# Pacing one scatter stream and moving additions, bias products and summing turns in a one-core graph-transformer kernel

## The chip, the cores and the metric

The kernel runs on one core of a Trainium2 chip, in fp32. The metric is the device time of one execution in microseconds (us), as the median of the runs of each kernel.

## The reference

A graph of 6250 nodes with 256 features and 100,000 weighted edges goes through two layers. `_L0_gnn_ref` and `_L1_gnn_ref` sum rows of neighbours, `_L0_mix_ref` is a linear attention with two layernorms, `_L1_mix_ref` a stack of four transformer layers with a linear attention, `_L0_ffn_ref` a mixture of 32 experts (top 1), `_L1_ffn_ref` one of 6 experts of width 256 (top 2, mixed by a softmax of the two scores).

```python
xn = _layernorm(x)
x = x + _L0_gnn_ref(xn, edge_index, edge_weight, ...) + _L0_mix_ref(xn[None], ...)[0]
x = x + _L0_ffn_ref(_layernorm(x)[None], ...)[0]
xn = _layernorm(x)
x = x + _L1_gnn_ref(xn, src, dst, deg_isqrt[:, None], weight) + _L1_mix_ref(xn[None], ...)[0]
x = x + _L1_ffn_ref(_layernorm(x)[None], ...)[0]     # sum over 2 of gate * (h2 @ W3[e] + b3[e])
```

## The kernel before, in words

The nodes are 50 tiles of T = 125 tokens. A loop iteration takes a pair of slots, each slot two tiles (250 tokens, a "chunk"), so NP = 13 iterations cover the NC = 25 chunks, the last with one slot only. Each engine has an instruction stream of its own; they meet at semaphores, and `Steps`/`KINDS` count the named steps of a phase (a name with ">" is done one iteration ahead).

The order of the work is this.

- **Sort, scatter(0).** DVE works out where every edge goes, twice (once per graph layer). POOL then sends the edges of the first sort to `scratch_sorted0` with 782 indirect DMAs of 128 records of 8 bytes (`scatter`, L975; EC = 782). At most `FLYING` of them are on their way: number c waits for c - FLYING to have landed. Beside this, PE, ACT and DVE do layer 0's attention (phases A0, B0).
- **Records.** SP loads the sorted records into `srec` (the names of tiles are those of the rows: `sb_srec`), DVE splits them into row numbers and targets (`take_records`, L1673 to L1676).
- **C0**, 25 iterations: POOL gathers 128 rows of `scratch_xn` at a time (`gather`, L982, NS = 880, a ring of RING = 8 tiles `sb_rows`), DVE makes a one-hot matrix of each, PE sums by a matmul with it (L2297), DVE adds the sum to its block (L1692). Beside it go the graph layer's MLP and the 32 experts. After every third gather (`BESIDE` = 3) POOL puts one scatter of the second sort, 293 in all; the other 489 follow in a tail behind C0, there with a memset of a spare tile behind each (`sb_rest`, L1010) as a pause. The tail's end is a load of `srec` (L1015) and a memset of the sums' 125 x 12850 tile (L1017).
- **A1.n, B1.n**, n = 0 to 3: the four layers. A1.n makes the context, B1.n the rest. From B1.1 on, each iteration carries three "turns" of the second graph sum: a turn is 8 gathers (L982), the one-hots (L1627), 16 matmul instructions (L2282), 4 additions (L1637) into `SUM[1]` (`sb_FREE`). 110 turns are due; B1.1 and B1.2 do 36 each, B1.3 the rest, two of them in its last iteration, which has one slot. DVE takes the records at the start of B1.1 (L1673 again).
- **C1**, written out over pairs j with the steps skewed (`C1_PE`, `C1_ACT`, `C1_DVE` list the names). DVE forms h = xn1 + sum (L2052, tile KT, pair j+2), PE turns it by transposes (L2227, 8 of them), multiplies by the graph weight (L2236), DVE adds it to x2 + state, the sum "xa" (L2113, tile TM), giving x3 (L2037) and its layernorm z (L2091), PE multiplies z by the router (L2682, L2689), DVE picks the two experts and works out the rows, POOL scatters z to those rows of `scratch_zs` (L1030, 8 indirect DMAs per pair). z has a ring of two buffers (`ZR`): z(j+1) waits for the scatters of pair j-1, in its buffer, to have landed.
- **Experts**, 54 tiles of 256 rows sorted by expert: PE turns the tile (L2735), two hidden layers (L2722), two matmuls that put in the bias of the chosen expert (L2763, out of a one-hot column), the output layer (L2767).
- **End.** POOL gathers the results of the two experts of each token (L1050, 100 indirect DMAs of 125 rows), DVE adds them times the gate (L2217), SP stores.

What each step waits for in the code: `scatter` holds `pool.wait_ge(scattered[e][c % FLYING], 16 * (c // FLYING))`; the first gather needs `srec_taken` 4, that is the whole scatter(0) landed, loaded and taken; the first gather of the second pass needs `srec_taken` 8. A gather also needs its ring slot back from PE (`row_free`).

## Time and profile before

| what | us |
|---|---|
| median of 3 runs | 7180.03 (7178.28 to 7499.05) |
| the profiled execution's own time | 7168.51 |
| its span, first to last instruction | 7166.8 |
| PE busy | 5509.7 |
| DVE busy | 3387.8 |
| POOL busy | 3803.2 |

The rows below are from the profiled execution, so times within it add up to 7168.51, not to the median. In the rows of a timeline a line is its start, its length, and in brackets how long the engine had been idle before it and what ended that. In grouped rows "xN" is the number of instructions, then busy us, the mean of one in ns, and the idle time before them with what ended it.

### The profile page before, as it was taken

To read this page: it belongs to the slowest core of one execution; us is meant where nothing else is said; L and a number is where in the kernel's file an instruction comes from. 1 tells how busy PE (TensorE), PEld (TensorE's weight loads), DVE (VectorE), ACT (ScalarE), POOL (GpSimd) and SP (SyncE) were. 2 spreads that over 40 slices of the span, in tenths; PEclk is the share of its full clock that TensorE was granted. 3 is DMA by queue.
4 is the path that set the end of the run, shared out by engine and by line. 5 is a ranking of instruction groups with operands and counts; after the bars stand their busy time and mean duration, and the time that the engine had idled before them with its cause. 6 is when DMAs were issued, how large, how long until landed. Compare 5 with 4: busy or idle time off the path is not lost.

```text
span 7166.8 us, 87343 instructions
## 1 busy us (share of the span) xinstructions
PE 5509.7 (77%) x24743; PEld 4508.0 (63%) x24743; DVE 3387.8 (47%) x10012; ACT 1297.9 (18%) x2949; POOL 3803.2 (53%) x4056
## 2 busy tenths in 40 slices
PE   0356673017999999999889999999998999965990
PEld 0245552015666666667778878888887878854880
DVE  8776664013444444443744554446444644456222
ACT  0011110000111111111422331124111411111330
POOL 0655556766666666667888725530554045535006
PEclk9987886557999999999999999999999999976995
DMA  1122220022222222232110122221322122443224
GB/s 37 39 74 67 62 65 22 1 61 73 83 80 82 81 82 80 82 79 46 49 28 18 35 71 79 80 71 54 83 82 76 43 76 82 77 105 92 80 71 114
DMA packets 327764, 477.28 MB, mean 67 GB/s; under 512 B 106708, under 2 KB 248254, under 8 KB 327470
## 3 DMA queue, kind: packets, MB, share of 16 engines
q0 software_dynamic: 161136, 262.61, 14.8%
q1 hardware_dynamic: 166334, 211.17, 9.5%
q8 instruction: 133, 2.18, 0.1%
q14 instruction: 161, 1.32, 0.1%
HBM read 370.96 MB, written 102.33 MB: 66 GB/s over the span
## 4 chain that ended last, share of the span: by engine, by line
PE 60%; another core or an unknown queue 8%; DVE 7%; issue 7%; DMA 3%; POOL 2%; DVEq 1%; ACT 1%; SPq 1%; POOLq 0%; ACTq 0%
PE bank L2236 13%; PE bank L2247 13%; PE bank L2297 6%; PE bank L2282 5%; PE bank L2463 5%; PE bank L2442 5%; PE bank L2722 3%; PE bank L2588 2%; PE bank L2227 2%; PE bank L2767 1%; POOL scratch_zs L1030 1%; PE bank L2445 1%; POOL sb_HT L1050 1%; DMA sb_work_QT<-scratch_q 1%
## 5 line engine op out<-in xcount | busy, mean ns | idle before, releaser
L982 POOL DMA_INDIRECT sb_rows<-scratch_xn,sb_row_of x1760 | 1734.2, 985 | 1849.8 <-PE bank L2282 939.8
L975 POOL DMA_INDIRECT scratch_sorted<-sb_FREE x1564 | 1604.0, 1026 | 890.8 <-issue 372.6
L2247 PE MATMUL bank<-sb_work_FT,sb_W 128*128 128x250 f32 x4400 | 1012.7, 381 | 16.3 <-ACT sb_work_FT L1059 11.5
L1059 ACT ACTIVATE sb_HT<-bank,sb_cols 128x250 f32<-128x250 f32 x1333 | 548.7, 467 | 2358.1 <-PE bank L2445 751.5
L2247 PEld LDWEIGHTS bank<-sb_work_FT,sb_W 128*128 128x128 f32 x4400 | 849.6, 194 | 131.7 <-ACT sb_work_FT L1059 16.5
L2297 PE MATMUL bank<-sb_rows,sb_work_TM 128*125 128x257 f32 x1760 | 528.7, 424 | 500.7 <-DMA sb_rows<-scratch_xn,sb_row_of 372.4
L2236 PE MATMUL bank<-sb_W,sb_HT 128*125 128x256 f32 x4000 | 889.0, 380 | 3.1 <-ACT sb_HT L1059 2.7
L2236 PEld LDWEIGHTS bank<-sb_W,sb_HT 128*125 128x125 f32 x4000 | 751.0, 188 | 118.3 <-ACT sb_HT L1059 4.4
L2297 PEld LDWEIGHTS bank<-sb_rows,sb_work_TM 128*125 128x125 f32 x1760 | 335.3, 203 | 591.3 <-issue 505.7
L1692 DVE TENSOR_TENSOR sb_STATE<-sb_STATE,bank 125x257 f32 x440 | 185.1, 421 | 971.0 <-PE bank L2297 663.7
L1637 DVE TENSOR_TENSOR sb_FREE<-sb_FREE,bank 125x257 f32 x440 | 186.1, 423 | 746.3 <-PE bank L2282 449.8
L2282 PE MATMUL bank<-sb_rows,sb_work_TM 128*125 128x257 f32 x1760 | 454.4, 401 | 22.9 <-DVE sb_FREE L1637 7.0
L2442 PE MATMUL bank<-sb_work_FT,sb_FREE 128*128 128x250 f32 x1600 | 463.5, 414 | 9.9 <-issue 9.2
L2463 PE MATMUL bank<-sb_FREE,sb_HT 128*125 128x256 f32 x1600 | 408.6, 401 | 0.0
L2236 PE MATMUL bank<-sb_W,sb_work_FT 128*125 128x256 f32 x1600 | 390.3, 403 | 19.9 <-ACT sb_work_FT L1059 19.9
L2282 PEld LDWEIGHTS bank<-sb_rows,sb_work_TM 128*125 128x125 f32 x1760 | 337.5, 197 | 102.2 <-issue 27.6
L2236 PEld LDWEIGHTS bank<-sb_W,sb_work_FT 128*125 128x125 f32 x1600 | 315.6, 201 | 76.6 <-ACT sb_work_FT L1059 20.2
L2442 PEld LDWEIGHTS bank<-sb_work_FT,sb_FREE 128*128 128x128 f32 x1600 | 305.7, 203 | 90.4 <-issue 30.3
L2463 PEld LDWEIGHTS bank<-sb_FREE,sb_HT 128*125 128x125 f32 x1600 | 308.3, 198 | 56.3 <-issue 9.0
L1059 ACT ACTIVATE sb_work_FT<-bank,sb_cols 128x250 f32<-128x250 f32 x400 | 192.3, 567 | 827.5 <-PE bank L2227 811.2
L1050 POOL DMA_INDIRECT sb_HT<-scratch_ys,sb_srec x100 | 120.6, 1206 | 412.9 <-DMA scratch_ys<-sb_work_KT 382.7
L1683 DVE TENSOR_SCALAR sb_work_TM<-sb_iota_t,sb_srec 128x125 f32<-128x125 f32 x880 | 284.4, 378 | 0.0
(363 smaller groups left out, 6933.9 us busy)
## 6 DMA issues: line engine op xcount, KB each, us to landing
sb_rows<-scratch_xn,sb_row_of POOLq DMA_INDIRECT x1760
scratch_sorted<-sb_FREE POOLq DMA_INDIRECT x1564
scratch_qT<-sb_work_QF SPq DMA_DIRECT2D x100, 250.0 KB
sb_work_QF<-scratch_qT SPq DMA_DIRECT2D x100, 250.0 KB
sb_work_XC<-in_x SPq DMA_DIRECT2D x50, 250.0 KB
sb_work_ZT<-scratch_xn SPq DMA_DIRECT2D x50, 250.0 KB
sb_W<-in_L_mix_W SPq DMA_DIRECT2D x9, 1024.0 KB
sb_work_XC<-scratch_zs SPq DMA_DIRECT2D x28, 256.0 KB, 2.7
```

Of the source, the lines that this page charges most:

```text
L975: nc.gpsimd.indirect_dma_start(out=sorted_d[e], out_offset=bass.IndirectOffsetOnAxis(ap=pos[e][0:n, c:c + 1], axis=0), in_=rec[e][0:n, 2 * ...
L982: nc.gpsimd.indirect_dma_start(out=rows[:, t % RING, 0:D], out_offset=None, in_=table, in_offset=bass.IndirectOffsetOnAxis(ap=row_of[:, t: ...
L1050: nc.gpsimd.indirect_dma_start(out=GY[j % YRING][:, t, k, :], out_offset=None, in_=ys_d, in_offset=bass.IndirectOffsetOnAxis(ap=Y_AT[:, 2 ...
L1059: return nc.scalar.activation(dst, source, func, **k)
L1683: nc.vector.tensor_scalar(onehot[:, u % RING, :], iota_t[:], srec[:, u, 0:1], srec[:, u, 1:2], ALU.is_equal, ALU.mult).then_inc(onehot_mad ...
L2236: ins = nc.tensor.matmul(dst[:, t, :], source[:, k, T * t:T * t + T], w[:, k, :], start=(begin and k == k0 and t == 0), stop=(end and k == ...
L2247: ins = nc.tensor.matmul(dst[:, b, :], w[:, k0 + k, 128 * (b0 + b):128 * (b0 + b) + 128], source[:, k, :], start=(n == 0), stop=(n == 2 * ...
L2282: nc.tensor.matmul(PSUMS[u // 2 % 2][0:T, 0:D + 1], onehot[:, u, :], rows[:, u, :], start=(u % 2 == 0), stop=(u % 2 == 1)).then_inc(row_fr ...
L2297: nc.tensor.matmul(PSUMS[g % 2][0:T, 0:D + 1], onehot[:, u % RING, :], rows[:, u % RING, :], start=(u % 2 == 0), stop=(u % 2 == 1)).then_i ...
L2442: nc.tensor.matmul(acc[:, b, :], w0_up[:, k, at:at + 128], FT[j % 2][:, k, :], start=(k == 0), stop=False)
L2463: ins = nc.tensor.matmul(acc[:, t, :], HT[:, j % 2, (2 * p + b) % 4, T * t:T * t + T], w0_down[:, 2 * p + b, :], start=False, stop=(p == 7 ...
L2722: ins = nc.tensor.matmul(whole(dst)[:, b, :], w[:, k, 128 * b:128 * b + 128], source[:, k, :], start=(k == 0), stop=(k == 1))
```

## The change

1. `FLYING` goes from 2 to 4, and every scatter(0) gets a pause behind it (`pause`, a memset of 128 x 320 as in the tail). `BESIDE` goes from 3 to 4: 220 scatters of the second sort beside C0, 562 in the tail.
2. The summing turns begin with the third iteration of B1.1; the last iterations of B1.1 and B1.2 carry three turns too, so 110 are still done. `take_records(1)` moves from before B1.1 to its second begin.
3. B1.3 drops the layernorm statistics behind its result, and adds x2 to the state instead (loaded there); C1 has no h and no xa on DVE. PE adds xn1 and the sum itself: 16 matmuls with the identity that accumulate in pairs, in place of 8 transposes. PE's graph product of pair j+2 now waits for DVE's x3 of pair j+1.
4. `ZR` has three buffers: z(j+1) waits for the scatters of pair j-2.
5. The bias matmuls leave the expert tiles. Behind the last tile PE turns a matrix of gates (50 tiles of 125 x 8, placed by five DVE operations during the experts), ACT copies it, and PE multiplies it by the biases; DVE adds that to the state, one addition of 125 x 512 per chunk ahead of its four gate additions. Two route steps go.
6. `Y_AT` and the gathers of results have 128 rows instead of 125.

```diff
-BESIDE = 3
-FLYING = 2
+BESIDE = 4
+PACED = EC
+FLYING = 4
...
-C1_DVE = (named(1, "x3", "stats", "mean") + named(2, "h") + named(0, "logit", "lmax", "lsub") + named(1, *RSQRT)
+C1_DVE = (named(1, "x3", "stats", "mean") + named(0, "logit", "lmax", "lsub") + named(1, *RSQRT)
...
+TURNS_FROM = {"B1.1": 2}
...
+LAST_TURNS = TURNS[f"B1.{LAYERS - 1}"] - (_turns - NS // RING)
...
+            def pause(n):
+
+                if n:
+                    pool.wait_ge(rested, n)
+                nc.gpsimd.memset(rest[:], 0.0).then_inc(rested, 1)
+
             for c in range(EC):
                 scatter(0, c)
+                if c < PACED:
+                    pause(c)
...
+                    if phase == "B1.1" and isinstance(i, int) and i == TURNS_FROM[phase] - 1:
+                        dve.wait_ge(sums_zeroed, 1)
+                        take_records(1)
...
-                if j + 2 < NP:
-                    for s in (slots_of(j + 2)):
-                        wait(dve, (xn1_read[s], 16 * (j + 3)))
-                        ins = nc.vector.tensor_tensor(KT[s], ZT[s], SUM[1][:, 4 * (j + 2) + 2 * s:4 * (j + 2) + 2 * s + 2, 0:D],
-                                                      ALU.add)
-                    ins.then_inc(*c1_dve.add("h", j + 2))
...
-                    wait(pe, c1_dve.done("h", j + 2))
                     for s in (slots_of(j + 2)):
-                        ins = turn_tok(pfeat(PA[s]), KT[s])
+                        wait(pe, (xn1_read[s], 16 * (j + 3)))
+                        sums = SUM[1][:, 4 * (j + 2) + 2 * s:4 * (j + 2) + 2 * s + 2, 0:D]
+                        for k in range(2):
+                            for t in range(2):
+                                for n, part_of in enumerate((ZT[s], sums)):
+                                    ins = nc.tensor.matmul(pfeat(PA[s])[:, k, T * t:T * t + T],
+                                                           part_of[:, t, 128 * k:128 * k + 128], ident[0:T, 0:T],
+                                                           start=(n == 0), stop=(n == 1))
                     ins.then_inc(*c1_pe.add("hT", j + 2))
                     wait(pe, c1_act.done("hT", j + 2))
+                    if j + 1 >= 0:
+                        wait(pe, c1_dve.done("x3", j + 1))
...
-                    if j >= 1:
-                        wait(dve, (z_scattered[(j + 1) % 2], 64 * sum(len_of(i) for i in range((j + 1) % 2, j, 2))))
+                    if j + 1 >= ZN:
+                        wait(dve, (z_scattered[(j + 1) % ZN], 64 * sum(len_of(i) for i in range((j + 1) % ZN, j + 1, ZN))))
...
                     for u in range(2):
-                        nc.tensor.matmul(y[:, u, :], chosen[:, t:t + 1].to_broadcast([NEXP1, 128]), bexp1,
-                                         start=(u == 0), stop=False, skip_group_check=True)
...
             for j in range(NC):
+                dve.wait_ge(bias_made, j + 1)
+                nc.vector.tensor_tensor(XM[:, 2 * j:2 * j + 2, :], XM[:, 2 * j:2 * j + 2, :], ptok(BIASED[j % 4]), ALU.add)\
+                    .then_inc(gate_added, 1)
                 dve.wait_ge(y_gathered[j % YRING], 64 * (j // YRING + 1))
```

POOL from the end of scatter(0) to the first gathers of C0, before (`scratch_sorted0` and `1` are the two sorts' outputs, `sb_rows` the ring of gathered rows):

```order
L975 DMA scratch_sorted0<-sb_FREE 112640x2 x782
L994 MEMSET sb_W1 32x2048
L929 AFFINE_SELECT sb_W1<-sb_W1 32x2048 x2
L982 DMA sb_rows<-scratch_xn0,sb_row_of 128x256 x3
L975 DMA scratch_sorted1<-sb_FREE 112640x2
```

and of the change, from the last scatter of the first sort on:

```order
L991 DMA scratch_sorted0<-sb_FREE 112640x2
L1008 MEMSET sb_rest 128x320
L1018 MEMSET sb_W1 32x2048
L945 AFFINE_SELECT sb_W1<-sb_W1 32x2048 x2
L998 DMA sb_rows<-scratch_xn0,sb_row_of 128x256 x4
L991 DMA scratch_sorted1<-sb_FREE 112640x2
```

Each of the 782 scatters now has a memset behind it, and the scatters in C0 stand behind four gathers instead of three.

PE in C1, one pair before (`sb_HT` the router's hidden layer, `sb_work_KT` is h, `sb_work_FT` its transpose, the `bank` numbers are PSUM banks):

```order
L2689 MATMUL bank6<-sb_W0,sb_HT 125x6 x4
L2227 MATMUL bank0<-sb_ident,sb_work_KT 128x125 x4
L2227 MATMUL bank3<-sb_ident,sb_work_KT 128x125 x4
L2236 MATMUL bank1<-sb_W0,sb_work_FT 125x256 x4
L2236 MATMUL bank4<-sb_W0,sb_work_FT 125x256 x4
L2668 MATMUL bank7<-sb_srec,sb_lower 125x32
```

and of the change. Sixteen products stand for one pair in the place of the eight transposes, eight per slot; the fence has the last two of them and what follows:

```order
L2705 MATMUL bank3<-sb_ident,sb_work_ZT 128x125
L2705 MATMUL bank3<-sb_ident,sb_FREE 128x125
L2279 MATMUL bank1<-sb_W0,sb_work_FT 125x256 x4
L2279 MATMUL bank4<-sb_W0,sb_work_FT 125x256 x4
L2719 MATMUL bank7<-sb_srec,sb_lower 125x32
```

The transposes of the DVE's sum are replaced by products of xn1 (`sb_work_ZT`) and of the sums (`sb_FREE`) in turn into one bank.

PE in the expert loop, one tile before (`sb_work_XC` the loaded tile, `sb_work_FT`, `sb_work_QF` and `sb_work_QT` the three layers' inputs, `sb_srec` holds the one-hot column):

```order
L2735 MATMUL bank0<-sb_ident,sb_work_XC 128x128 x4
L2722 MATMUL bank4<-sb_work_FT,sb_W0 128x256 x4
L2722 MATMUL bank2<-sb_work_QF,sb_W0 128x256 x4
L2717 TENSOR_LOAD sb_srec
L2717 ISA x2
L2763 MATMUL bank7<-sb_W1,sb_srec 128x256 x2
L2767 ISA
L2767 MATMUL bank7<-sb_FREE,sb_work_QT 128x256 x2
L2767 ISA
L2767 MATMUL bank7<-sb_FREE,sb_work_QT 128x256 x2
```

and of the change:

```order
L2786 MATMUL bank3<-sb_ident,sb_work_ZT 128x128 x4
L2773 MATMUL bank1<-sb_work_FT,sb_W0 128x256 x4
L2773 MATMUL bank5<-sb_work_QF,sb_W0 128x256 x4
L2768 TENSOR_LOAD sb_srec
L2768 ISA x2
L2815 ISA
L2815 MATMUL bank6<-sb_FREE,sb_work_QT 128x256
L2815 ISA
L2815 MATMUL bank6<-sb_FREE,sb_work_QT 128x256 x3
```

The two bias products are gone from every tile, and nothing stands in their place there.

## Rows read from the trace of the kernel before

**Rows 1.** The page: busy time and share, and the sum matmuls of C0.
```profile
PE 5509.7 (77%) x24743; PEld 4508.0 (63%) x24743; DVE 3387.8 (47%) x10012; ACT 1297.9 (18%) x2949; POOL 3803.2 (53%) x4056
...
L2297 PE MATMUL bank<-sb_rows,sb_work_TM 128*125 128x257 f32 x1760 | 528.7, 424 | 500.7 <-DMA sb_rows<-scratch_xn,sb_row_of 372.4
```

**Rows 2.** Busy time by stretch: PE, PEld, DVE, ACT, POOL, then clock, DMA share, GB/s.
```profile
1172.00:1518.00 346.00, 1.62 (x2) 0.08 (x2) 13.95 (x12) 0.00 (x0) 261.54 (x270) 0.50 0.02 1
1640.00:3240.00 1600.00, 1441.54 (x5928) 1075.85 (x5926) 686.02 (x2589) 203.77 (x480) 1038.60 (x1072) 0.91 0.30 81
3617.00:4008.00 391.00, 383.60 (x1815) 335.18 (x1813) 162.26 (x496) 103.50 (x242) 342.06 (x500) 0.99 0.07 15
...
6374.00:6590.00 216.00, 145.72 (x599) 117.13 (x599) 152.97 (x692) 34.54 (x85) 106.07 (x88) 0.70 0.35 103
6630.00:7000.00 370.00, 369.95 (x1716) 297.62 (x1716) 80.65 (x210) 122.63 (x270) 0.00 (x0) 1.00 0.23 74
7010.00:7160.00 150.00, 0.00 (x0) 0.00 (x0) 40.90 (x98) 0.00 (x0) 117.00 (x97) 0.50 0.48 125
```

**Rows 3.** Groups by line, POOL, stretches 240:700, 700:1160, 3331:4083 (two).
```profile
L975 POOL DMA_INDIRECT scratch_sorted<-sb_FREE x222 | 240.2, 1082 | 218.5 <-DMA scratch_sorted<-sb_FREE 170.6 <-issue 47.9
...
L975 POOL DMA_INDIRECT scratch_sorted<-sb_FREE x234 | 265.7, 1135 | 196.0 <-DMA scratch_sorted<-sb_FREE 139.9 <-issue 56.1
...
L975 POOL DMA_INDIRECT scratch_sorted<-sb_FREE x464 | 457.8, 987 | 117.1 <-issue 73.5 <-DMA scratch_sorted<-sb_FREE 43.5
L1010 POOL MEMSET sb_rest<- 128x320 f32 x465 | 178.2, 383 | 0.3
```

**Rows 4.** Timeline of POOL: scatter(0)'s end, C0's first gather, C0's end, the clearing behind the tail.
```profile
1516.92 1.04 POOL L975 DMA_INDIRECT scratch_sorted<-sb_FREE  x1 [0.30 <-issue]
1532.09 1.04 POOL L982 DMA_INDIRECT sb_rows<-scratch_xn,sb_row_of  x1 [0.17 <-issue]
...
3292.04 0.99 POOL L975 DMA_INDIRECT scratch_sorted<-sb_FREE  x1 [0.30 <-issue]
...
4085.81 10.83 POOL L1017 MEMSET sb_FREE<- 125x12850 f32 x1
```

**Rows 5.** Timeline of DVE: the records taken, for C0 and for B1.1.
```profile
1523.70 0.62 DVE L1673 TENSOR_SCALAR sb_row_of<-sb_srec 128x880 f32<-128x880 f32 x1 [331.50 <-DMA sb_srec<-scratch_sorted]
...
4214.68 0.62 DVE L1673 TENSOR_SCALAR sb_row_of<-sb_srec 128x880 f32<-128x880 f32 x1 [0.89 <-DMA sb_work_QF<-scratch_qT]
```

**Rows 6.** Timeline of PE: iterations of B1.0 and B1.1, B1.3's last iteration.
```profile
3652.27 4.07 PE L2247 MATMUL bank<-sb_work_FT,sb_W 128*128 128x250 f32 x18 [0.67 <-ACT sb_work_FT L1059]
...
3684.86 4.49 PE L2247 MATMUL bank<-sb_work_FT,sb_W 128*128 128x250 f32 x20 [0.58 <-ACT sb_work_FT L1059]
...
4305.48 3.62 PE L2236 MATMUL bank<-sb_MM,sb_work_QF 128*125 128x256 f32 x16
...
4352.05 3.62 PE L2236 MATMUL bank<-sb_MM,sb_work_QF 128*125 128x256 f32 x16
...
6307.89 0.94 PE L2282 MATMUL bank<-sb_rows,sb_work_TM 128*125 128x257 f32 x2 [0.79 <-DMA sb_rows<-scratch_xn,sb_row_of]
```

**Rows 7.** C1: timeline of PE, then DVE's groups by line, 6374:6590.
```profile
6466.02 6.68 PE L2236 MATMUL bank<-sb_W,sb_work_FT 128*125 128x256 f32 x16 [1.15 <-ACT sb_work_FT L1059]
...
6483.92 1.05 PE L2227 MATMUL bank<-sb_ident,sb_work_KT 125*128 125x125 f32 x8
...
L2052 DVE TENSOR_TENSOR sb_work_KT<-sb_work_ZT,sb_FREE 125x512 f32<-125x512 f32 x19 | 12.7, 705 | 0.3
L2091 DVE TENSOR_SCALAR sb_work_QT<-sb_STATE,sb_MV,sb_RY 125x256 f32<-125x256 f32 x22 | 7.6, 409 | 23.5 <-DMA scratch_zs<-sb_work_QT,sb_srec 23.5
L2091 DVE TENSOR_SCALAR sb_W<-sb_STATE,sb_MV,sb_RY 125x256 f32<-125x256 f32 x20 | 6.9, 409 | 13.6 <-DMA scratch_zs<-sb_W,sb_srec 13.6
```

**Rows 8.** Experts 6630:7000 and the end: groups by line.
```profile
L2763 PE MATMUL bank<-sb_W,sb_srec 6*128 6x256 f32 x216 | 60.7, 400 | 0.0
...
L1050 POOL DMA_INDIRECT sb_HT<-scratch_ys,sb_srec x97 | 117.0, 1206 | 29.6 <-issue 26.5 <-DVE sb_STATE L2217 3.1
```

More of the change, by code:

```diff
@@ L270, in pairs, with pairs_next @@
     body(NP - 1, (0,))
-def pairs_next(engine, begin, body):
+def pairs_next(engine, begin, body, phase=None):
     begin(0, (0, 1))
-    body(0, (0, 1), (0, 1))
-    with engine.Fori(1, NP - 2) as i:
+    written_out = max(1, TURNS_FROM.get(phase, 0))
+    for i in range(written_out):
+        body(i, (0, 1), (0, 1))
+    with engine.Fori(written_out, NP - 2) as i:
         body(i, (0, 1), (0, 1))
@@ L492, in build @@
         tilesT, beganT, endedT = (carve(1, 8) for _ in range(3))
[L493 removed]
+        ended = carve(NX, NEXP1)
         exp_row, real, tile_in = (carve(NX, 1) for _ in range(3))
@@ L555, in build @@
         gate_added, out_stored = sem("gate_added"), sem("out_stored")
+        gates_placed, gates_turned, gates_copied, bias_made = (
+            sem(n) for n in ("gates_placed", "gates_turned", "gates_copied", "bias_made"))
         routing_cleared, y_placed = sem("routing_cleared"), sem("y_placed")
-        ROUTE_STEPS = ["tiles", "whole", "began", "ended", "done", "begun", "chosen", "row", "real", "in", "rel", "in0",
+        ROUTE_STEPS = ["tiles", "whole", "began", "ended", "done", "row", "real", "in", "rel", "in0",
                        "last", "exp_of", "in_of"]
@@ L853, in load_b1 @@
                                      .rearrange("u p (k n) -> p (u k) n", k=2)).then_inc(q_loaded.sems[s], 16)
+                    if phase == f"B1.{LAYERS - 1}":
+                        for s in slots:
+                            if not first(i):
+                                wait(sp, dve_done.done(phase, "xa", i - 1, s))
+                            sp.dma_start(XC[s], tiles(x2_d)[:, bass.ds(4 * i + 2 * s, 2), :]).then_inc(x2_read.sems[s], 16)
                 pairs_late(sp, load_b1, load_for_next)
@@ L882, in _ @@
                     sp.dma_start(dst, source).then_inc(weights_loaded["exp_rest"], 16)
-                wait(sp, c1_dve.done("xa", j))
-                for s in (slots_of(j + 1)):
-                    load_x2(j + 1, s)
             weight_loads["exp_rest"] = 16 * 2 * NEXP1
-            for s in range(2):
-                sp.wait_ge(z_scattered[s], 64 * sum(len_of(j) for j in range(s, NP, 2)))
+            for q in range(ZN):
+                sp.wait_ge(z_scattered[q], 64 * sum(len_of(j) for j in range(q, NP, ZN)))
             sp.wait_ge(pads_scattered, 16 * 2 * NEXP1)
@@ L1007, in _ @@
                 scatter(1, c)
-                if c > ahead_of:
-                    pool.wait_ge(rested, c - ahead_of)
-                nc.gpsimd.memset(rest[:], 0.0).then_inc(rested, 1)
+                pause(PACED + c - ahead_of)
             for mark in all_scattered(1):
@@ L1258, in _ @@
                     relu_tile(b, "b", H2, PC, 1)
+            for q in range(NP):
+                n = T * 2 * len_of(q)
+                act.wait_ge(gates_turned, q + 1)
+                if q >= 2:
+                    act.wait_ge(bias_made, 2 * (q - 1))
+                move(GT[q % 2][:, 0:n], PA[q % 2][0:8, 0:n]).then_inc(gates_copied, 1)
         @block.vector
@@ L1968, in body_b1 @@
                             .then_inc(*dve_done.add(phase, "b2", slots, s))
+                    if phase == f"B1.{LAYERS - 1}":
+                        for s in slots:
+                            self_wait(phase, "b2", i, s)
+                            wait(dve, x2_read.done(phase, i, s))
+                            nc.vector.tensor_tensor(state(i, s), state(i, s), XC[s], ALU.add)\
+                                .then_inc(*dve_done.add(phase, "xa", slots, s))
+                        return
                     for s in slots:
@@ L2033, in body_c1 @@
                 if 0 <= j + 1 < NP:
-                    wait(dve, c1_dve.done("xa", j + 1))
                     wait(dve, c1_pe.done("gnn", j + 1))
@@ L2179, in _ @@
                 dve.wait_ge(weights_loaded[name], weight_loads[name])
-            for s in range(2):
-                dve.wait_ge(z_scattered[s], 64 * sum(len_of(j) for j in range(s, NP, 2)))
+            for q in range(ZN):
+                dve.wait_ge(z_scattered[q], 64 * sum(len_of(j) for j in range(q, NP, ZN)))
             of_tile = {}
```

117 lines of the change are left out of this document (72 added, 45 removed).

## The prediction

> **What bounds the kernel now.** The page first: PE is busy 77% of the span, POOL 53%, and one line of PE, the sum matmuls of C0, has waited 372.4 us once for gathered rows [rows 1]. No engine is full throughout, so each stage has to be read for its own limit.
>
> The table of stretches gives it [rows 2]. In 1172:1518 PE does 1.62 us of work and POOL 261.54: nothing goes on but scatter(0). The timelines show how it ends: last scatter at 1516.92, DVE takes the records at 1523.70 after 331.50 idle, the first gather is at 1532.09 [rows 4, 5]. In C0 (1640:3240) PE has 1441.54 of 1600, at clock 0.91; in the attention layers (3617:4008) 383.60 of 391; in the experts (6630:7000) all of it. [...] In the end (7010:7160) POOL has 117.00 of 150 and nobody else comes near [rows 2].
>
> So: POOL bounds from about 1165 to 1532 and the last 150 us, PE nearly all the rest, and C1 a chain. A saving on POOL in A1 or B1, or on DVE there, is worth nothing.
>
> **The change, part by part.** The terms are added to the profiled execution's own 7168.51 us. The comparison runs of the same kernel have a median of 7180.03, 11.5 more; I give the sum as it comes from the profile.
>
> *Scatter(0).* While the attention runs, 222 scatters take 240.2 + 218.5 us, 2.07 each; 234 take 265.7 + 196.0, 1.97 each [rows 3]. Of this 170.6 and 139.9 are waits for a landing: with two in flight, number c waits for c - 2. Four in flight leave 4 x 1.7 = 6.8 us for a landing where now some 4 are given, so I take those waits as gone. The added memset costs 0.383 [rows 3], and the gap before a scatter is then 73.5/464 = 0.16 [rows 3]. Scatter 1.11 (mean of the two stretches) + 0.16 + 0.38 = 1.65; I take 1.70, for contention. In quiet, the tail of before shows 457.8 + 73.5 + 178.2 us for 464, without its landing waits: 1.53. Now: 42 scatters are done by 240 us as before, 925/1.70 = 544 by 1165, and the other 196 take 300 us: the end is at 1465, not 1517. C0 starts with it: **-52**. Bounds: at 1.65 the end is 1439 (-78); if the waits stay as they are, 2.02 each, it is 42 + 458, then 282 x 1.53 = 431, end 1596 (+79). What the memset costs DVE in A0 and B0 has 370 us of idle PE behind it.
>
> [...] In 3617:4008 POOL did 250 memsets beside 250 scatters and PE still had 383.60 of 391 [rows 2]; nothing shows that memsets harm a neighbour. [...]
>
> *C0.* From 1532.09 to 3292.04 are 25 iterations of 70.4 us [rows 4]. POOL has 1038.60 us of work in 1600 [rows 2] and loses 73 scatters; it has room either way. PE's rest, 158 us in 1600, is spread over waits that the views don't put on gathers. Only the first 100 us, while the ring fills, go by POOL's pace: a fourth gather in place of a scatter now and then, 6 scatters of 1.3 us. **-8**, bounds 0 and -158 (the whole of PE's rest in that stretch gone).
>
> *Tail of scatter(1).* 562 instead of 489. Before, 1.62 each with all waits: (457.8 + 117.1 + 178.2)/464 [rows 3]; without landing waits 1.53. From 3292 it ends between 4152 and 4204; then the load is issued and the sums are cleared, over at 4085.81 + 10.83 = 4096.6 [rows 4], 13 us behind the tail's end (3292 + 489 x 1.62 = 4084). DVE needed the records at 4214.68 [rows 5]; now one half iteration later, about 4231. Margin 14 to 66 us: **0**.
>
> *B1 turns.* An iteration without turns takes 3684.86 - 3652.27 = 32.6 us, one with three 4352.05 - 4305.48 = 46.6 [rows 6]: a turn is 4.66. Six turns leave the first two iterations of B1.1 (-28) and six enter two last iterations with one slot. There a turn has half as much beside it: B1.3's last one, with two turns, waits for gathers in between (0.79 in the row [rows 6]). I take 6.3 each, +38. **+10**, bounds 0 and +25.
>
> *B1.3 and C1's start.* B1.3 loses the statistics and gains two additions per iteration on DVE, which has slack. C1's first loads are two of 250 KB instead of four: **-3**.
>
> *C1.* The stretch 216 us holds 88 scatters, 11 pairs: 19.6 us per pair. DVE waits 23.5 + 13.6 = 37.1 us in it for a scatter to have left the z buffer, 3.4 per pair [rows 7]. With three buffers that goes, and POOL's 8 scatters (106.07/88 + 0.30 = 1.5 each, 12 per pair) don't bound. DVE is left with 16.2, less two pairs of 0.7 (L2052, and L2113 of the same form) [rows 7]: 13.4. PE: busy 13.2 per pair at clock 0.70, so some 9.3 at full clock. The 16 added products have 16 x 125 columns, about as many as the 8 products of 256 columns that take 3.62 at full clock and 6.68 at half [rows 6, 7]; less the transposes' 1.05, +2.5. Four waits for ACT of 1.15 [rows 7] give 4.6. Sum 16.4 at full clock, 18.6 + 5.5 + 4.6 = 28.7 at half. PE becomes C1's bound. I take 16.4 with a little at half: 12 periods x -3.2 = **-38**. Bounds: -12 x 6.2 = -74 (DVE alone) and 12 x 9.1 = +109 (all at half clock).
>
> [...]
>
> *Experts.* Four instructions per tile leave, 60.7 us as recorded [rows 8], 4/32 of 6.85 us per tile by count, which is 46 over 54 tiles. PE is full there [rows 2] and DVE and ACT, 80.65 and 122.63 of 370, have room. I take **-57**. The new transposes and products at the end fill a wait that POOL's gathers set; DVE gets one addition of 125 x 512 per chunk, 0.7 by the like one in rows 7, where it has 40.90 busy of 150.
>
> *End.* 97 gathers of 125 rows take 1206 ns each [rows 8], the indirect DMAs of 128 rows 987 in the tail [rows 3]. The 0.30 between them stays: 100 x 0.22 = **-22**, bounds 0 and -25.
>
> Sum: -52 - 8 + 0 + 10 - 3 - 38 - 57 - 22 = -170, so 7168.5 - 170 = **6998 us**.
>
> **Rivals.**
>
> *(a) The pause costs more than the flights give.* If landings aren't what holds POOL but the transfers' own pace, the period stays 2.02 with the memset inside: +79 instead of -52, 7129. For it: 1.97 to 2.07 while the DMAs are busy. Against: 310 us of the idle is named as a landing wait, and only 104 as issue.
>
> *(b) C1 at half clock.* +109 instead of -38: 7145; half of it 7072. For it: clock 0.70 now, four waits per pair. Against: PE is busier per pair than before (12 of 16 instead of 13 of 20).
>
> *(c) C0's rest goes.* If PE's 158 us come from late gathers after all, a third less scatter work in between lets most go: -110 instead of -8, 6896. Against: POOL is no more than 65% busy.
>
> *(d) The bias products weren't the bound.* If the tiles wait for their loads once PE is faster, -57 becomes 0: 7055. Against: DMA share 0.23.
>
> *(e) The tail comes late, slower than before.* DVE takes the records at the second begin of B1.1, and everything behind it on DVE and PE waits. From 1.65 us per scatter (4231 - 13 - 3292 = 926 over 562) this bites, at 5.6 us per 0.01. At 2.07, as beside A0 [rows 3], the tail ends 3292 + 1163 = 4455, 237 late: 7235, slower. For it: no more than 0.03 between 1.623 and 1.65. Against: beside A1 the transfers are few (15 GB/s [rows 2]), and four flights take the landing waits off.
>
> **How the numbers follow.** Chances: the forecast 0.60, (a) 0.09, (b) 0.14, (c) 0.07, (d) 0.05, (e) 0.05. The forecast's own range is 6955 to 7040. The whole range leaves out the far half of (c), most of (a) and (e) and the worst of (b): 6920 to 7110. A measurement of this kernel tells about 2% from no change, a bound of 7025 on the profile's own base. Forecast and (c) lie mostly below it, with 27 us to spare: faster 0.62. (a), (b), (d) and what the forecast misses by more than that: same 0.35. A case that is 2% slower needs (e) and (a) together: 0.03.
>
> **What would show it.** Right: scatter(0) ends near 1465, without landing waits in A0 and B0; the first gather near 1480; tail's load of records before 4180 in old time; C1's groups of scatters 16 to 17 us apart with PE, not the z ring, as releaser and a clock above 0.9; expert tiles at 5.8 us; final gathers 1.3 us apart. Wrong: landing waits that stay in scatter(0), a granted clock of 0.5 through C1, an idle DVE ahead of the second taking of records, or a C0 iteration off 70 us by more than 1.

## The result, and the profile after

The changed kernel takes 6965.57 us (median of 4 runs, 6947.83 to 6978.54); the kernel before took 7181.57 in the same comparison. The ratio is 0.9699, its 95% interval 0.9672 to 0.9726: 3.0% faster. Some runs of the kernel before are slow ones (here 7499.05 us, one of four, and three of seven on the second chip below), and neither the ratios nor the medians below rest on such runs. The profiled execution of the changed kernel took 6978.54 us, against 7168.51: 190 us less, where 170 had been forecast.

The page of the changed kernel, busy time and the sum matmuls of C0 (now line 2340), answers to [rows 1]:

```profile
PE 5457.0 (78%) x24977; PEld 4497.6 (64%) x24977; DVE 3425.7 (49%) x9891; ACT 1306.8 (19%) x2962; POOL 4109.6 (59%) x4911
...
L2340 PE MATMUL bank<-sb_rows,sb_work_TM 128*125 128x257 f32 x1760 | 511.2, 417 | 322.9 <-DMA sb_rows<-scratch_xn,sb_row_of 276.5
```

The wait for C0's first gathered rows is still the longest of PE, 276.5 instead of 372.4 us: 63 of the 96 us less come from an earlier C0, the rest from PE ending layer 0's attention later. POOL is busier by 306 us; the 855 memsets more, at about 0.39 us each, account for it. The stretches that answer to [rows 2], of the changed kernel (PE, PEld, DVE, ACT, POOL, clock, DMA share, GB/s):

```profile
1172.00:1458.00 286.00, 14.97 (x54) 10.79 (x54) 32.46 (x61) 2.19 (x4) 253.83 (x375) 0.52 0.03 5
1580.00:3100.00 1520.00, 1378.73 (x5852) 1045.84 (x5852) 677.63 (x2541) 203.27 (x476) 949.82 (x984) 0.94 0.30 83
6297.00:6492.00 195.00, 141.89 (x851) 122.56 (x850) 137.00 (x696) 35.02 (x87) 116.47 (x100) 0.88 0.35 96
6520.00:6815.00 295.00, 295.00 (x1469) 259.88 (x1468) 81.79 (x211) 119.63 (x264) 0.00 (x0) 1.00 0.28 89
6830.00:6960.00 130.00, 45.98 (x116) 26.14 (x114) 49.57 (x109) 5.19 (x9) 91.45 (x94) 0.50 0.46 138
```

C1's clock has gone from 0.70 to 0.88; the experts are as full as before and shorter; in the last stage POOL is busy 91.45 us of 130, where it was 117.00 of 150.

POOL's scatters of the first sort, groups by line in 240:700 and 700:1160, answer to [rows 3]:

```profile
L991 POOL DMA_INDIRECT scratch_sorted<-sb_FREE x273 | 289.1, 1059 | 65.0 <-issue 41.9 <-DMA scratch_sorted<-sb_FREE 23.1
...
L991 POOL DMA_INDIRECT scratch_sorted<-sb_FREE x271 | 295.9, 1092 | 55.6 <-issue 43.6 <-DMA scratch_sorted<-sb_FREE 11.9
```

273 in 460 us is one every 1.69 us, and the landing waits are down from 170.6 and 139.9 us to 23.1 and 11.9. The timelines of POOL (the last scatter, the first gather, the clearing of the sums) and of DVE (the second taking of records) answer to [rows 4, 5]:

```profile
1458.09 0.88 POOL L991 DMA_INDIRECT scratch_sorted<-sb_FREE  x1 [0.17 <-issue]
...
1469.01 1.00 POOL L998 DMA_INDIRECT sb_rows<-scratch_xn,sb_row_of  x1 [4.00 <-DVE sb_row_of L1705]
...
4020.40 10.84 POOL L1039 MEMSET sb_FREE<- 125x12850 f32 x1
...
4129.39 0.61 DVE L1702 TENSOR_SCALAR sb_row_of<-sb_srec 128x880 f32<-128x880 f32 x1
```

The last thing that the second taking of records waits for was done 98 us before it (4031.2 to 4129.4), so the longer tail costs nothing.

Where did the 190 us come from? The starts of the first or last instruction of each stage, read from the views of single lines, give this table. The right half is from two later runs of the same two kernels on another chip, told below.

| stretch | before | after | difference | before, 4th chip | after, 4th chip | difference |
|---|---|---|---|---|---|---|
| start to first gather of C0 | 1532.1 | 1469.0 | -63.1 | 1520.8 | 1462.3 | -58.5 |
| to C0's last sum matmul | 1774.1 | 1704.3 | -69.8 | 1502.9 | 1488.9 | -14.0 |
| to the last addition of a turn | 3004.8 | 3066.3 | +61.5 | 2901.4 | 2920.5 | +19.1 |
| to the first scatter of z | 63.4 | 56.7 | -6.7 | 62.8 | 55.9 | -6.9 |
| to the last scatter of z | 232.2 | 195.6 | -36.6 | 230.2 | 195.6 | -34.6 |
| to the first expert matmul | 22.2 | 22.0 | -0.2 | 22.0 | 22.1 | +0.1 |
| to the last expert matmul | 372.9 | 305.4 | -67.5 | 374.1 | 305.3 | -68.8 |
| to the last gate addition | 159.0 | 152.5 | -6.5 | 160.0 | 134.8 | -25.2 |

So on the first chip three terms were far from the forecast: C0 gave 70 instead of 8, the turns cost some 60 instead of 10, and the end gave 6.5 instead of 22. The first two nearly cancel. The experiments went after these three, and after the two halves of the first edit.

### The profile page after: what moved, and what is told of

Same layout as the page of the kernel before. It is cut to its first block, busy times and chain, and to the rows that moved or that the text cites. A ratio compares the mean times of both kernels' runs of the same rounds, so it can differ in the third digit from the quotient of the medians.

```text
span 6976.8 us, 88468 instructions
## 1 busy us (share of the span) xinstructions
PE 5457.0 (78%) x24977; PEld 4497.6 (64%) x24977; DVE 3425.7 (49%) x9891; ACT 1306.8 (19%) x2962; POOL 4109.6 (59%) x4911
## 4 chain that ended last, share of the span: by engine, by line
PE 60%; POOL 15%; DVE 8%; issue 7%; DMA 5%; another core or an unknown queue 4%; DVEq 1%; ACT 1%; SPq 0%; ACTq 0%; POOLq 0%
PE bank L2279 14%; PE bank L2290 13%; POOL scratch_sorted L991 10%; PE bank L2325 6%; PE bank L2340 5%; PE bank L2506 5%; PE bank L2485 4%; POOL sb_rest L1008 4%; DMA scratch_sorted<-sb_FREE 3%; PE bank L2773 3%; PE bank L2631 3%; PE bank L2270 2%; PE bank L2815 1%; DMA sb_rows<-scratch_xn,sb_row_of 1%
## 5 line engine op out<-in xcount | busy, mean ns | idle before, releaser
L2340 PE MATMUL bank<-sb_rows,sb_work_TM 128*125 128x257 f32 x1760 | 511.2, 417 | 322.9 <-DMA sb_rows<-scratch_xn,sb_row_of 276.5
L1008 POOL MEMSET sb_rest<- 128x320 f32 x1344 | 523.6, 390 | 1.0
L2485 PE MATMUL bank<-sb_work_FT,sb_FREE 128*128 128x250 f32 x1600 | 439.5, 398 | 0.3 <-issue 0.3
L2279 PE MATMUL bank<-sb_W,sb_work_FT 128*125 128x256 f32 x1600 | 366.2, 385 | 21.2 <-ACT sb_work_FT L1081 13.2
L2279 PEld LDWEIGHTS bank<-sb_W,sb_work_FT 128*125 128x125 f32 x1600 | 297.9, 190 | 69.7 <-issue 13.2
L2506 PEld LDWEIGHTS bank<-sb_FREE,sb_HT 128*125 128x125 f32 x1600 | 304.7, 196 | 56.7 <-issue 10.7
L1072 POOL DMA_INDIRECT sb_HT<-scratch_ys,sb_srec x100 | 97.9, 979 | 355.2 <-DMA scratch_ys<-sb_work_KT 314.8
```

The costliest lines, as they stand in the source:

```text
L1008: nc.gpsimd.memset(rest[:], 0.0).then_inc(rested, 1)
L2279: ins = nc.tensor.matmul(dst[:, t, :], source[:, k, T * t:T * t + T], w[:, k, :], start=(begin and k == k0 and t == 0), stop=(end and k == ...
L2340: nc.tensor.matmul(PSUMS[g % 2][0:T, 0:D + 1], onehot[:, u % RING, :], rows[:, u % RING, :], start=(u % 2 == 0), stop=(u % 2 == 1)).then_i ...
L2485: nc.tensor.matmul(acc[:, b, :], w0_up[:, k, at:at + 128], FT[j % 2][:, k, :], start=(k == 0), stop=False)
L2506: ins = nc.tensor.matmul(acc[:, t, :], HT[:, j % 2, (2 * p + b) % 4, T * t:T * t + T], w0_down[:, 2 * p + b, :], start=False, stop=(p == 7 ...
```

## The experiments

Twelve kernels were run, four to a chip; each chip also ran the kernel before. The kernel before took 7142 us (median) on the second chip, 6783.09 on the third, 6787.21 on the fourth, where the first had 7180. This difference of 5.0 to 5.5% is larger than the change, and it turned out to sit just where the forecast had missed. So I compare stages within a chip where I can, else between the first and the second or between the third and the fourth, which are alike, and across chips only ratios.

**Fewer scatters beside C0, alone and taken back (second chip).**

```diff
-BESIDE = 3
+BESIDE = 4
```
in the kernel before, and `BESIDE = 3` in the changed kernel.

> The kernel before with BESIDE = 4 alone (one scatter of the second sort behind every fourth gather, 562 of them in the tail). C0, from its first sum matmul to its last, took 1768 us before and 1698 in the changed kernel. Theory A, fewer scatters between the gathers give this: C0 takes about 1700 here, the whole is 55 to 70 us faster than before, 7110 to 7125. Theory B, the four flights give it (a scatter no longer holds POOL until an earlier one has landed): C0 stays within 10 us of 1768, the whole within 15 us of before.

> The changed kernel with BESIDE = 3. Theory A: C0 goes back to about 1765 and the whole is 55 to 70 us slower than the changed kernel, about 7030. Theory B: C0 stays at 1698 within 10, the whole at 6966 within 15. If both parts count, each of the two runs shows some half of the 70.

The kernel before with `BESIDE = 4` took 7065.56 us, ratio 0.9894 (0.9854 to 0.9933), and C0, from its first sum matmul to its last, 1680.9 us. The changed kernel with `BESIDE = 3` took 6982.13, ratio 0.9775 (0.9741 to 0.9808), C0 1750.2. All three kernels of this chip with `BESIDE = 4` (this one and those of the next two experiments) have 1675.5 to 1685.5, so C0 is 65 to 75 us shorter with it; on the first chip it was 1768.2 before and 1697.5 in the changed kernel. Theory A stands: the number of scatters beside C0 is what counts, at 0.9 to 1.0 us for each of the 73. The flights (how many scatters may be on their way) show no effect on C0: the 1680.9 is with two, the other two kernels have four.

**The turns put back (second chip).**

```diff
-TURNS_FROM = {"B1.1": 2}
+TURNS_FROM = {}
```
with the records taken before B1.1 and the last iterations of B1.1 and B1.2 without turns, as in the kernel before.

> The changed kernel with the summing turns where they were before (from B1.1's first iteration, none in the last iterations of B1.1 and B1.2). From the last sum matmul of C0 to the last addition of a turn before took 3004.8 us, in the changed kernel 3066.3, 61 more, of which the moved turns were to give 10. Theory C, the moved turns cost it: this stretch goes back to about 3005 and the whole is 55 to 60 us faster than the changed kernel, about 6907. Theory D, the iterations fall into a 43 us or a 47.4 us pattern by chance, whatever the turns: the stretch is shorter by the 10 to 25 us that the turns themselves cost, and the count of 47 us iterations does not go back to 20 of 36.

It took 6898.92 us, ratio 0.9661 (0.9623 to 0.9699), the fastest of that chip. The stretch from C0's last sum to the last turn took 3014.0 us, against 3044.0 and 3047.1 in the two kernels of this chip with moved turns. So moving them costs 30 to 33 us here, half of theory C's 61 and more than theory D's 10 to 25. Where it goes can be read from the starts of the iterations, on the first chip: the last, single-slot iterations of B1.1 and B1.2 take 18 to 20 us more each (234.4 and 233.1 instead of 214.8 and 214.7 from the iteration before to the first of the next layer), +38; the first two of B1.1 take 33.5 and 32.6 instead of 45.0 and 46.4, -25. Most of the rest is slow iterations. On these chips a B1 iteration takes either some 43 or some 47 us, and the three kernels with moved turns had 24, 22 and 21 of 34 at over 45.5, the three others 19, 21 and 19 of 36. PE's timeline of the changed kernel shows what a slow one has:

```profile
5049.45 1.74 PE L2270 MATMUL bank<-sb_ident,sb_work_ZT 125*128 125x125 f32 x8 [2.69 <-DVE sb_work_ZT L1336]
5051.29 3.00 PE L2325 MATMUL bank<-sb_rows,sb_work_TM 128*125 128x257 f32 x8
```

PE waits 2.69 us for DVE's normalised tile; then the granted clock is 0.50 (in 5050:5053; 0.99 in the 2 us before, 1.00 from 5054 on), the 8 transposes take 1.74 instead of 1.05 us and the next 8 matmuls 3.00 instead of 1.90. The wait and the half clock make 4.5 us, about what lies between the two kinds. Why DVE's tile is late in them is not shown.

**No pause, four flights (second chip).**

```diff
-PACED = EC
+PACED = 0
```

> The changed kernel with four flights but no pause behind the scatters of the first sort. Theory E, the pause pays for itself by spacing the scatters: without it scatter(0) is not sooner than 1458 us. Theory F, the pause only adds its 0.38 + gap and the landing waits are gone by the flights: a scatter takes 1.11 + 0.30 = 1.41 instead of 1.69 beside A0 and B0 and 1.26 behind, so scatter(0) ends at about 172 + 50 x 1.39 + 925 / 1.41 and is done near 1250 us, C0 starts some 200 us earlier, bounded by the end of B0 at about 1170, and the whole is some 200 us faster than the changed kernel. In between, landing waits with four flights decide: at 1.97 us as before, the end is 1517 again and the whole is 60 us slower.

It took 7500.4 us, ratio 1.0501 (1.0466 to 1.0536): 5% slower than the kernel before. Neither theory had this. The scatters did go faster, the last was issued at 1239.6, as F said. But C0's first gather came at 2038.5. Beside the scatters layer 0's attention nearly stood still. The stretch 240:700 of this run, then of the changed kernel:

```profile
240.00:700.00 460.00, 68.11 (x199) 47.96 (x200) 71.22 (x172) 10.75 (x22) 348.47 (x346) 0.58 0.06 13
```
```profile
240.00:700.00 460.00, 242.36 (x1078) 207.25 (x1078) 324.46 (x709) 68.57 (x140) 394.95 (x546) 0.79 0.23 65
```

PE did 68 us of work instead of 242, the DMAs moved 13 GB/s instead of 65, and the DMA engines were busy 6% of the time: they were not full. The timeline of the run without pauses shows who was held up:

```profile
653.62 0.16 DVE L1302 TENSOR_TENSOR sb_RT<-sb_RY 125x4 f32<-125x4 f32 x1 [2.63 <-issue]
653.86 1.10 POOL L991 DMA_INDIRECT scratch_sorted<-sb_FREE  x1 [0.30 <-issue]
655.10 0.59 ACT L1081 ACTIVATE sb_work_FT<-bank 128x500 f32<-128x500 f32 x1 [56.14 <-remote]
655.27 1.09 POOL L991 DMA_INDIRECT scratch_sorted<-sb_FREE  x1 [0.30 <-issue]
...
657.11 0.16 DVE L1303 TENSOR_TENSOR sb_RT<-sb_RT,sb_RV 125x4 f32<-125x4 f32 x1 [3.34 <-issue]
```

The little operations of DVE's inverse root, each 0.16 us long and waiting only for the one before it, start 2.1 to 3.5 us apart, about two scatters, where in the kernel before they follow every 0.27. The profile puts the gaps before them (1.95 to 3.34 us in 653:677) down to "issue" and names no data and no DMA that they wait for; meanwhile POOL issues indirect DMAs back to back, mostly 0.30 us apart. What is late in the step from one instruction to the next is not shown, nor whether the issuing does it or the landings, which come as densely. ACT and PE have long gaps too (56.14 us and, at 655.81, 51.32), with no releaser named; that they have the same cause is likely, not shown. In the kernel before, the waits for a landing, 170.6 and 139.9 us in two stretches of 460 [rows 3], had broken POOL's stream; in the changed kernel, with four flights, they are 23.1 and 11.9, and the pause has to do it. The memsets have a price of their own on DVE. One of its operations in 240:1160, in the kernel before and in the changed one:

```profile
L1307 DVE TENSOR_SCALAR sb_work_ZT<-sb_work_XC,sb_MV,sb_RY 125x256 f32<-125x256 f32 x50 | 17.5, 412 | 2.5 <-DVE sb_RY L1275 2.1 <-issue 0.2
```
```profile
L1336 DVE TENSOR_SCALAR sb_work_ZT<-sb_work_XC,sb_MV,sb_RY 125x256 f32<-125x256 f32 x50 | 25.3, 564 | 2.5 <-DVE sb_RY L1304 2.1 <-issue 0.2
```

It takes 564 ns instead of 412, and a little one of 125x4 (now L1300) 535 instead of 193; without pauses they take 420 and 170. The TENSOR_TENSOR operations of the inverse root stay at 163 to 166, and the TENSOR_SCALAR of the same line and shape that reads a PSUM bank at 537 and 538. DVE's 1714 instructions in 160:1458 take 747 us instead of 698, and PE's last work ahead of C0's sums ends at 1209.1 instead of 1177.7; how much of that is the memsets' part is not separated. Why some operations become longer beside the memsets and others do not is not shown. It costs the whole nothing, since PE then still waits 267 us for C0's rows. Without the pauses DVE did 71 us of work in 460 instead of 324.

**Pause with two flights (third chip).**

```diff
-FLYING = 4
+FLYING = 2
```

> The changed kernel with two scatters in flight and the pause kept. Theory K, with the pause two flights do as well as four: scatter(0) ends within 10 us of 1458. Theory L, the flights took the landing waits off: at 1.97 to 2.07 us per scatter beside A0 and B0 it ends at about 1590, the whole is 130 us slower than the changed kernel; if a part of the waits stays, in between. C0 should stay at 1676 to 1698 in both.

It took 6783.49 us, ratio 0.9995 (0.9985 to 1.0004): all that the rest of the change gains is lost. Scatter(0)'s last was issued at 1655.3 instead of 1452. POOL's group in 240:700:

```profile
L991 POOL DMA_INDIRECT scratch_sorted<-sb_FREE x203 | 216.0, 1064 | 166.0 <-DMA scratch_sorted<-sb_FREE 140.0 <-issue 25.8 <-DVE sb_STATE L1401 0.2
```

The landing waits are all back, 140.0 us, 0.69 per scatter, and the pause comes on top: 2.27 us per scatter, more than theory L's 2.07 (it had taken the pause to lie inside the waits). C0 took 1480.9, as in the kernels of this chip with four flights (1481.6 and 1483.4): flights do nothing there. With the run before, the first edit is settled: pause and flights are worth something only together. C0's first gather is 54 to 63 us earlier with both than with neither (1467.7 and 1470.6 against 1524.8 on the second chip), 145 us later with the pause alone (1666.2 against 1520.8 on the fourth), 514 later with the flights alone (2038.5 against 1524.8).

**Pauses elsewhere (third and fourth chip).** All with the turns where they were; a pause is the same memset behind the instruction.

```diff
-                gather(1, xn1_d, t)
+                gather(1, xn1_d, t); pause(PACED + EC - ahead_of + t)
```

> The changed kernel with the turns where they were before (as in the run of the moved turns), and a pause (the memset of 128 x 320) behind each of the 880 gathers of the second sum. Theory G, POOL's DMA instructions back to back hold up the semaphores and instructions of the other engines, and the 47 us iterations of B1.1 to B1.3 come from that: with the pause most of the 36 iterations fall to 43 us, the stretch from the last sum of C0 to the last turn is 50 to 90 us shorter than 3014. Rival H, the 47 us pattern is PE's and DVE's own: nothing changes within 15 us, or the stretch grows because 24 gathers of 1.5 us leave less room.

```diff
-                    scatter(1, t // BESIDE)
+                    scatter(1, t // BESIDE); pause(PACED + t // BESIDE)
```

> The same base, with a pause behind each of the 220 scatters in C0. Theory G: C0 (1675 in the base) shrinks, by up to 60 us, since each scatter would hold PE up less. Rival I, a scatter in C0 costs its own POOL time, because gathers are late by it: the pause adds up to 220 x 0.24 us, C0 takes 1690 to 1730.

```diff
-                            .then_inc(y_gathered[j % YRING], 16)
+                            .then_inc(y_gathered[j % YRING], 16); pause(PACED + EC - ahead_of + 4 * j + 2 * t + k)
```

> The same base, with a pause behind each of the 100 final gathers. A gather then takes 1.50 instead of 1.255 us, 25 us more of POOL. In the changed kernel ACT copied two of its 13 gate tiles 28 and 15 us after PE had turned them, with no releaser that the profile names, and POOL then waited 9.3 us. Theory G: those gaps go, POOL never waits, and the final stage takes 149.7 + 25 - (9 to 14), 160 to 166 us. Rival J, the gaps are instruction loads of ACT: they stay where they are, and the stage takes 170 to 175.

The ratios are 0.9776 (0.976 to 0.9793) with the pause in B1, 0.9730 (0.9714 to 0.9746) in C0, 0.9735 (0.9719 to 0.9752) at the end. What was to be cured did not occur on this chip: without a pause its B1 iterations take 42.4 us, nearly every one, and C0 1483.4. So each pause only cost its time: B1's stretch 2947.8 instead of 2904.6 and 2907.1 in the other two, C0 1498.4 instead of 1483.4, the end 158.3 instead of 135.8. For theory G in C0 and B1 these runs decide nothing; that a pause is not free is what they show. A fourth kernel had the pauses in C0 and in B1 together:

> The turns where they were, with a pause behind each scatter in C0 and each gather of the second sum. Theory G (POOL's DMA instructions back to back hold up the other engines) gives on a chip like the first C0 and B1 at the pace of the third chip or near it: C0 down by 100 or more from 1676 and B1's iterations at 43 to 44, the whole 100 us or more faster than the changed kernel. Rival H: C0 within 20 us of 1690, B1's iterations still at 43 and 47. On a chip like the third both say 15 us more in C0 and 40 more in B1, as in the two runs that had one of the pauses each.

It fell on the fourth chip, like the third, and took 6643.81 us, ratio 0.9787 (0.9771 to 0.9804), C0 1497.1: the price again, and no verdict.

**The two kernels again, on the fourth chip.**

> The kernel before, unchanged, profiled on the same chip as the next three. The chips differ: on the first and second one the kernel before took 7180 and 7164 us, on the third 6783, and there C0 with BESIDE = 4 took 1482 to 1498 us and the iterations of B1 42.4, instead of 1676 to 1698 and 43 to 47. Theory M, the chip decides C0 and B1 and nothing else: on a chip like the third C0 is near 1510 here and B1's iterations 42.4, every other stage as in the rows of before; on a chip like the first all is as in them.

> The changed kernel, unchanged, on that chip. Scatter(0) should end at 1453 to 1458 on any chip, C1 be some 37 us shorter than in the run of before, the experts 67. C0: 53 to 87 us shorter than before on a chip like the first; on one like the third, where it runs at PE's pace (98% busy), no more than 20 to 30. From C0's last sum to the last turn: 13 us longer than before on a chip like the third (the turns alone), 30 to 60 on one like the first.

6787.25 and 6594.49 us; the second's ratio is 0.9714 (0.9697 to 0.9730). The stages are in the right half of the table above. Theory M stands, with one addition: besides C0 and B1 the end differs, 134.8 instead of 152.5 us in the changed kernel, while it takes 160.0 and 159.0 in the kernel before. All others agree within 5 us, but for the start (6.7 to 11). C0's stretches of the two kernels, before first:

```profile
1640.00:2960.00 1320.00, 1290.88 (x5799) 990.52 (x5800) 662.81 (x2507) 204.44 (x475) 1003.75 (x1038) 1.00 0.35 95
```
```profile
1580.00:2900.00 1320.00, 1294.20 (x5850) 998.68 (x5849) 674.87 (x2533) 206.32 (x480) 942.83 (x979) 1.00 0.36 95
```

PE is 98% busy at full clock in both, so scatters taken out of C0 give only 14 us. On the first chip the same code had PE at 90% with clock 0.91 [rows 2]. Rows that come late are not the reason there. A gather is 32 packets of 4096 bytes; past the first 40 gathers PE stood 34 times for more than 0.3 us ahead of a sum matmul, 55 us in all, and each time the last packet of its rows had ended 4.2 us or more before. On the fourth chip it stood so 17 times, 19 us, and the middle one of these was 0.39 us behind the packet.

The end on the first chip, ACT's and POOL's timeline of the changed kernel, and ACT's on the fourth:

```profile
6904.67 0.58 ACT L1081 ACTIVATE sb_work_FT<-bank 8x500 f32<-8x500 f32 x1 [33.02 <-remote]
...
6910.72 0.95 POOL L1072 DMA_INDIRECT sb_HT<-scratch_ys,sb_srec  x1 [9.32 <-DVE sb_STATE L2251]
```
```profile
6497.92 0.58 ACT L1081 ACTIVATE sb_work_FT<-bank 8x500 f32<-8x500 f32 x1 [10.54 <-PE bank L2827]
```

On the first chip PE had turned the gates at 6876.4 and ACT copied them 28 us later, with nothing in the profile that released it and no packet of kind "instruction" in between (so rival J has no support); DVE then lacked the biases, and POOL a free buffer for 9.32 us. On the fourth every copy follows PE's transposes at once. The second chip's runs with this code have an end of 149.7 to 152.2, like the first's.

**Still fewer scatters beside C0 (fourth chip).**

```diff
-BESIDE = 4
+BESIDE = 5
```
with the turns where they were.

> The turns where they were, BESIDE = 5 (176 scatters beside C0, 606 in the tail). On a chip like the first: 44 scatters fewer in C0 at 0.7 to 1.2 us each shorten C0 by 30 to 50; the tail is 44 x 1.53 = 67 us longer, and in the run of the moved turns it had 54 us before the records were taken, so the whole is 0 to 35 us faster than the changed kernel with the turns where they were (6899). On one like the third C0 gains less than 10, and the tail's surplus comes late: the whole is 10 to 30 us slower than with BESIDE = 4.

6599.2 us, ratio 0.9721 (0.9705 to 0.9738), with C0 at 1480.3, no gain, and the tail late. Timelines of POOL, DVE and PE:

```profile
3869.59 10.83 POOL L1039 MEMSET sb_FREE<- 125x12850 f32 x1
```
```profile
3880.66 0.62 DVE L1702 TENSOR_SCALAR sb_row_of<-sb_srec 128x880 f32<-128x880 f32 x1 [25.01 <-POOL sb_FREE L1039]
```
```profile
3892.52 1.93 PE L2271 MATMUL bank<-sb_ident,sb_work_ZT 125*128 125x125 f32 x8 [30.41 <-DVE sb_work_ZT L1336]
```

This is rival (e) in small: DVE waits for the clearing behind the tail, PE for DVE, and B1.1's first iteration takes 68.0 us instead of 43 to 45.

## Why the prediction was right, point by point

The forecast was 6998 us, 170 less than the profiled 7168.5, with a range of 6920 to 7110; it is 6965.57, and 190 less between the profiled executions.

*Scatter(0), -52: right, by its mechanism.* 1.69 us per scatter where 1.70 was taken, end at 1458 where 1465 was, first gather 63 us earlier. Of the 11 us more than forecast, 7 are the earlier end and 4 the masks behind the last scatter, which POOL now makes while the records are on their way. What I had not seen is how much hung on the pause: I had priced it as a cost of 0.38 us with contention at the most, and without it the kernel is 5% slower than before. "Nothing shows that memsets harm a neighbour" was a wrong reading: in the tail of the kernel before DVE's L1307 already took 565 ns (3617:4008) and 410 behind it (4214:4780). The 370 us of idle PE covered it, as the forecast had it. Rival (a), that the waits stay 2.02, occurs with two flights only, and then it is 2.27.

*C0, -8: wrong in size on the first chip, near on the fourth (-14).* The step that failed is "PE's rest, 158 us in 1600, is spread over waits that the views don't put on gathers", from which I took that fewer scatters would not touch it. The bound (-158) held, the value did not: 70 of it went. Rival (c) had the right place, though not the cause, since the rows of the gathers had come 4.2 us or more before PE's waits. The two runs with one edit each put it on the number of scatters.

*Tail, 0: right*, with a margin of 98 us where 14 to 66 were given; C0's extra gain moved both ends of it. Rival (e) was shown with `BESIDE = 5`.

*Turns, +10: too low on the first two chips, right by luck on the fourth.* The stretch grew by 61.5 us between the two profiled executions, by 30 to 33 through the turns alone on the second chip, by 19 on the fourth. On the fourth the two last iterations cost 28 us where 38 was forecast, and B1.1 up to its last iteration lost 17.5 where 28 was: +10.7, two errors of 10 that cancel. The step that failed is "a turn is 4.66": an iteration with three turns takes 42.4 there, so a turn is 3.3. The 4.66 was read from an iteration of the slow kind [rows 6] and held the wait (2.12 us at 4321.57) and the half clock (0.50 in 4322:4325) in it. Another 5.7 us of the 19 lie in B1.3 (514.1 to 519.8 from its first iteration to its last) and not with the turns, for the kernels of the third and fourth chip that have them put back, and no pause in B1, show 519.9 to 520.6: there "two additions per iteration on DVE, which has slack" was put at nothing. On the first two chips the slow iterations also grew in number, which no step had.

*B1.3 and C1's start, -3:* C1's start gives 6.7 to 6.9, B1.3 takes back the 5.7 just told.

*C1, -38: right*, 34.6 to 36.6. 195.6 us for 100 scatters is 15.6 per pair where 16.4 was worked out, and the 232.2 of before is 18.6 where 19.6 was read, so the difference held though both ends were one too high. POOL's and DVE's part is as said: DVE's z operations no longer wait (idle 0.1 in the view by line). PE's part too: in 6297:6492 its instructions make up some 63% of the chain of work that ended last, and its clock rose (0.88, where above 0.9 was forecast). On C1's timeline of the changed kernel the waits that are left are ACT's copies:

```profile
6388.50 3.72 PE L2279 MATMUL bank<-sb_W,sb_work_FT 128*125 128x256 f32 x16 [1.67 <-ACT sb_work_FT L1081]
...
6395.27 1.96 PE L2733 MATMUL bank<-sb_work_QF,sb_W 128*128 128x250 f32 x8 [1.16 <-ACT sb_work_QF L1081]
```

The graph product takes 3.72 us, not 6.68 as in the row of before [rows 7]. Its granted clock was 1.00 (6388.50:6392.20), where the row of before had 0.50 (6467:6472). Rival (b), C1 at half clock, did not come: with waits of 0.9 to 1.7 us on this timeline the mean clock of 6297:6492 was 0.88, between the 0.50 and the 1.00 of other stretches. What takes it below 1.00 is not shown.

*Experts, -57: right in kind, 10 too small.* 67.5 to 68.8, that is 1.25 us per tile. I had discounted the recorded 1.12 for overlap; the whole of it went, and some of what lay around it. Rival (d) did not come.

*End, -22: right on the fourth chip (-25.2), -6.5 on the first*, where "fill a wait that POOL's gathers set" failed: ACT's copy of the gates came late and the chain PE, ACT, PE, DVE held POOL.

The total was right partly because two misses on the first chip, C0 and B1, had opposite signs: 62 us too little and 51 too much. On the fourth chip the forecast's own basis, the sum over terms without such stalls, comes out at -188 for -170 with every term within 12.

What stays open is what makes C0, B1 and the end slower on two chips. All three are places where POOL issues indirect DMAs close together, in C0 PE waits although its rows have come 4.2 us or more before, and in the run without pauses, on such a chip, PE did 68 us of work and DVE 71 in 460 beside a dense stream of them, instead of 242 and 324. That makes it the likeliest cause. It is not shown: the kernels with pauses in these places fell on chips that do not have the stalls, and the one without pauses ran only on a chip that has them. That the rows there name no releaser ("issue", "remote") is no evidence. On the first two chips the trace lacks about half of the records of DMA landings (31,544 updates for the kernel before on the first chip, 66,169 on the fourth), so that "issue" and "remote" can hide one. The page shows it in the gathers, which have no time to landing on the first chip and 2.8 us on the fourth:

```profile
sb_rows<-scratch_xn,sb_row_of POOLq DMA_INDIRECT x1760
```
```profile
sb_rows<-scratch_xn,sb_row_of POOLq DMA_INDIRECT x1760, 2.8
```

Whether the same thing loses the records and makes the stalls is open too.

## What to carry to other kernels

A stream of indirect DMAs from POOL is not free for the other engines because it lies beside them (beside 346 scatters in 460 us PE did 68 us of work, beside 273 with a pause behind each 242): count them, and leave gaps in it by something that is known, not by a wait that a later edit may remove. When a wait is about to go, ask what it was protecting besides its buffer; here two edits that look like rivals (more in flight, a pause behind each) are worth some 60 us together and cost 514 and 145 alone. A pause made of memsets has a price of its own on DVE (564 ns instead of 412 for one of its operations here), so it belongs where DVE has room. And take the price of a step from an iteration without a stall, by looking at several of them: 32.6 and 46.6 us gave 4.66 for a turn, where 42.4 gives 3.3.

## What the runs showed of the hardware

The same kernel takes 7142 to 7180 us on two chips and 6783 to 6787 on two others, a difference of 5.0 to 5.5%. It does not lie in the clock of a full PE, for the experts take 372.9 and 374.1 us on the first and fourth, but in C0 (1768 and 1496 from the first sum matmul to the last), in B1 (43 to 47 us an iteration, and 42.4), and in the changed kernel in its last stage (152.5 and 134.8). The change is worth 3.0% on the first and 2.9% on the fourth, by different stages.

Beside scatters of 128 records of 8 bytes, one every 1.33 us (346 in 460 us), the other engines did a fraction of their work on the one chip where this was run: PE 68 us, DVE 71 and ACT 10.75 of the 460, against 242, 324 and 68.57 in the changed kernel on the first chip. DVE's dependent operations went from 0.27 us apart to 2.1 to 3.5, and the DMAs moved 13 GB/s in all, with the DMA engines 6% busy. With one every 1.69 us and a memset of 0.39 us behind each, PE did 242 us of work in the same 460, and 261 in the kernel before.

With a POOL memset of 128 x 320 behind every scatter DVE's TENSOR_SCALAR of 125 x 256 (`sb_work_ZT<-sb_work_XC`) took 564 ns, against 412 in the kernel before and 420 without the pauses. The one that reads a PSUM bank stayed at 537 and 538, and the TENSOR_TENSOR operations of 125 x 4 at 163 to 166.
